# Linear attention and a binarised convolution on one core: keys in pairs, two banks' statistics on ScalarE, stores spread over three queues

## What is computed

```python
def _L0_conv_ref(x, g, b, w_qkv, w_out, b_out):      # 8 heads of 32
    mean, var = jnp.mean(x, axis=1, keepdims=True), jnp.var(x, axis=1, keepdims=True)
    xn = (x - mean) / jnp.sqrt(var + EPS) * g + b    # over the channels
    qkv = jnp.einsum('bchw,oc->bohw', xn, w_qkv).reshape(B, 3, HEADS, DIM_HEAD, N)
    q, k, v = qkv[:, 0] * scale, jax.nn.softmax(qkv[:, 1], axis=-1), qkv[:, 2]
    context = jnp.einsum('bhcn,bhdn->bhcd', k, v)
    out = jnp.einsum('bhcd,bhcn->bhdn', context, q).reshape(B, HEADS * DIM_HEAD, H, W)
    return jnp.einsum('bchw,oc->bohw', out, w_out) + b_out[None, :, None, None] + xn

def _L1_conv_ref(x, W, gamma, beta):
    y = lax.conv_general_dilated(jnp.sign(x), jnp.sign(W), (1, 1), ((1, 1), (1, 1)), ...)  # 3 x 3
    mean, var = jnp.mean(y, axis=(0, 2, 3)), jnp.var(y, axis=(0, 2, 3))
    inv = gamma / jnp.sqrt(var + BN_EPS)
    return (y - mean) * inv + beta + x               # per channel
```

## Time and profile before

| | us |
|---|---|
| median of 3 runs (104.31 to 104.75) | 104.68 |
| profiled execution: its own time | 104.13 |
| profiled execution: its span | 102.3 |

### The profile page before, as it was taken

How to read it: one execution, slowest core, us unless ns; L and a number is a source line. 1 busy time by engine, 2 the same in 40 slices (tenths; PEclk the granted TensorE clock), 3 DMA queues, 4 the chain that set the end, 5 groups by cost and what they waited for, 6 DMA issues and landing times.

```text
span 102.3 us, 2028 instructions
## 1 busy us (share of the span) xinstructions
PE 83.5 (82%) x768; PEld 46.7 (46%) x771; DVE 57.8 (56%) x116; ACT 55.1 (54%) x103; POOL 27.3 (27%) x38
## 2 busy tenths in 40 slices
PE   4999988999997999999999999999999998100000
PEld 4942423556563556455666457565554453100000
DVE  4817959743399345576891684115216299559500
ACT  2246957588894567276792727875214250298000
POOL 6996462462482712082400000000000000005000
PEclk9999999999999999999999999999999999985555
DMA  2997023033000321000240003500800908003993
GB/s 54 308 340 279 10 71 121 0 100 108 0 3 0 103 64 44 0 0 0 72 136 0 0 0 83 128 0 0 205 6 10 201 13 192 0 0 77 319 314 111
DMA packets 4876, 8.89 MB, mean 87 GB/s; under 512 B 1430, under 2 KB 1746, under 8 KB 4868
## 3 DMA queue, kind: packets, MB, share of 16 engines
q1 hardware_dynamic: 3604, 7.59, 25.8%
q10 hardware_dynamic: 1104, 0.66, 2.4%
q0 software_dynamic: 160, 0.52, 1.5%
HBM read 2.51 MB, written 2.10 MB: 45 GB/s over the span
## 4 chain that ended last, share of the span: by engine, by line
PE 69%; DVE 15%; ACT 5%; issue 3%; DVEq 1%
PE ps L791 15%; PE ps L777 8%; PE ps L682 6%; PE ps L778 6%; DVE ST L605 5%; PE ps L849 4%; PE ps L830 3%; PE ps L900 3%; PE ps L743 3%; PE ps L697 3%; PE ps L805 3%; PE ps L812 3%; DVE mxp L532 2%; PE ps L731 2%; PE ps L718 2%
## 5 line engine op out<-in xcount | busy, mean ns | idle before, releaser
L392 ACT ACTIVATE E<-ps 128x512 f32<-128x512 f32 x32 | 18.2, 594 | 5.2 <-PE ps L778 5.2
L532 DVE TENSOR_REDUCE mxp<-ps 128x2 bf16<-128x1024 f32 x12 | 14.7, 1224 | 10.5 <-PE ps L743 10.2
L777 PE MATMUL ps<-wk_max,S 128*128 128x256 bf16 x64 | 15.7, 276 | 0.5 <-ACT wk_max L345 0.5
L791 PE MATMUL ps<-E,XT 128*64 128x256 f32 x128 | 15.6, 385 | 0.0
L778 PE MATMUL ps<-wk_lo,S 128*128 128x256 bf16 x64 | 15.5, 273 | 0.0
L308 POOL DMA_DIRECT2D out<-OUT x2 | 1.3, 674 | 43.2 <-DVE OUT L672 43.2
L791 PEld LDWEIGHTS ps<-E,XT 128*64 128x64 f32 x128 | 8.5, 136 | 4.7 <-issue 0.8
L279 POOL TENSOR_TENSOR x_lo<-XN,x_hi 128x512 bf16<-128x512 f32 x8 | 9.2, 1155 | 2.3 <-DVE x_hi L515 2.2
L321 ACT ACTIVATE sq<-ps 128x512 f32<-128x512 f32 x8 | 4.8, 597 | 8.4 <-PE ps L682 8.4
L682 PE MATMUL ps<-X,center_mat 128*128 128x512 f32 x16 | 9.0, 668 | 0.3 <-DVE XN L509 0.3
L777 PEld LDWEIGHTS ps<-wk_max,S 128*128 128x128 bf16 x64 | 6.2, 97 | 5.9 <-issue 2.8
(11 more groups left out here) (115 smaller groups left out, 130.1 us busy)
## 6 DMA issues: line engine op xcount, KB each, us to landing
X<-in_x SPq DMA_DIRECT2D x3, 512.0 KB, 5.2
X<-X SPq DMA_DIRECT2D x4, 256.0 KB, 3.5
X<-X SPq DMA_DIRECT2D x8, 128.0 KB, 2.4
out<-OUT SPq DMA_DIRECT2D x4, 256.0 KB, 4.1
S<-x_hi SPq DMA_DIRECT2D x7, 126.0 KB
S<-x_lo SPq DMA_DIRECT2D x7, 126.0 KB
X<-in_x SPq DMA_DIRECT2D x2, 256.0 KB, 3.8
out<-OUT POOLq DMA_DIRECT2D x2, 256.0 KB, 4.5
```

Of the source, the lines that this page charges most:

```text
L392: nc.scalar.activation(E[:, b % 2, 2 * g:2 * g + 2, :].rearrange("p k j -> p (k j)"), kt_ps[g % 2], ACT.Exp).then_inc(exp_ready, 1)
L532: nc.vector.tensor_reduce(mxp[:, h, :, t], k_ps, AX.X, ALU.max).then_inc(max_ready, 1)
L777: nc.tensor.matmul(dst, chunk, wk_max[:, b % 2, :], start=True, stop=False)
L791: last = nc.tensor.matmul(d_ps[d * C:d * C + C, :], XT[:, b, k, :], E[:, b % 2, k, :], start=(k < 2), stop=(k >= CH - 2))
```

## The change

TensorE's order: from image 0 on, keys_t is called in pairs (groups 0 and 1, then 2 and 3) with half_keys, project and others between pairs; first_keys(1, 0) stands ahead of keys_t(0, 0); the first rows (pair 0) go to bank 7 and no longer to bank 0, with new waits on the copies that read bank 7; apply_matrix(1) moves from image 7 to the end of image 6. ScalarE's order follows: keep_pt(2) and keep_pt(4) move ahead of the row copies, and the copy of the query and value weights ahead of the second row. VectorE does first_max(1, 0) before normalise(3), and add_input(1) before scale_r(5).

The ending: banks 2 and 3 are no longer among VectorE's statistics. ScalarE reads them in one pass that sums, and in a second that squares the difference from the mean and sums; it writes mean and sum of squares in the form of the statistics' records, whose counts GpSimd writes. SCALED and ADDED begin with banks 4 and 5 singly. The stores are 12 instead of 10: 6 on SP, 5 on GpSimd, 1 on ScalarE.

```diff
-SCALED = ((4, 5), (6, 7), (1,), (0,), (2,), (3,))
-ADDED = ((4, 5), (6, 7), (0, 1), (2,), (3,))
+SCALED = ((4,), (5,), (6, 7), (1,), (0,), (2,), (3,))
+ADDED = ((4,), (5,), (6, 7), (0, 1), (2,), (3,))
+ACT_STATS = (2, 3)
+RECORDS = 4
...
+acc = sb("acc", [P, 3])
+ACC_SUM, ACC_MEAN, ACC_SQUARES = (acc[:, i:i + 1] for i in range(3))
...
+def row_ps(q):
+    return ps[:, 0 if q else 7, 0:HID]
...
-conv_done, y_ready, st_ready = sem("conv_done"), sem("y_ready"), sem("st_ready")
+conv_done, y_ready, st_ready, st_act = sem("conv_done"), sem("y_ready"), sem("st_ready"), sem("st_act")
+st_counts = sem("st_counts")
...
+act_records = ST[:, ACT_STATS[0]:ACT_STATS[-1] + 1, :].rearrange("p b (r e) -> p (b r) e", e=3)
...
-for pair in ((4, 5), (6, 7)):
-    wait_added(sp, pair)
-    sp.dma_start(out_h[0, :, pair[0]:pair[1] + 1, :], OUT[0:C, pair[0]:pair[1] + 1, :]
+for part in ((4,), (5,), (6, 7)):
+    wait_added(sp, part)
+    sp.dma_start(out_h[0, :, part[0]:part[-1] + 1, :], OUT[0:C, part[0]:part[-1] + 1, :]
...
-for q in two:
-    sp.dma_start(out_d[2 * q], OUT[q * C:(q + 1) * C, 0:2, :]).then_inc(stored, 16)
+sp.dma_start(out_d[0], OUT[0:C, 0:2, :]).then_inc(stored, 16)
+wait_added(sp, (2,))
+sp.dma_start(out_d[1, :, 0:BANK], OUT[0:C, 2, :]).then_inc(stored, 16)
...
-sp.wait_ge(stored, 16 * 8)
-sp.wait_ge(stored_pool, 16 * 2)
+sp.wait_ge(stored, 16 * 7)
+sp.wait_ge(stored_pool, 16 * 5)
...
-for pair in ((4, 5), (6, 7)):
-    wait_added(pool, pair)
-    pool.dma_start(out_h[1, :, pair[0]:pair[1] + 1, :], OUT[C:P, pair[0]:pair[1] + 1, :]
+nc.gpsimd.memset(act_records[:, :, 0:1], float(len(ACT_STATS) * BANK // RECORDS)).then_inc(st_counts, 1)
+for part in ((4,), (5,), (6, 7)):
+    wait_added(pool, part)
+    pool.dma_start(out_h[1, :, part[0]:part[-1] + 1, :], OUT[C:P, part[0]:part[-1] + 1, :]
...
+wait_added(pool, (0, 1))
+pool.dma_start(out_d[2], OUT[C:P, 0:2, :]).then_inc(stored_pool, 16)
+wait_added(pool, (3,))
+pool.dma_start(out_d[3, :, BANK:N], OUT[C:P, 3, :]).then_inc(stored_pool, 16)
...
-    nc.scalar.copy(wk_max[d * C:d * C + 1, d, :], ps[d * C:d * C + 1, 0, 0:HID]).then_inc(row_ready, 1)
+    nc.scalar.copy(wk_max[d * C:d * C + 1, d, :], row_ps(b // 2)[d * C:d * C + 1, :]).then_inc(row_ready, 1)
...
-    if b >= 2:
+    if b in (2, 3, 5, 7):
...
-    if b == 1:
-        keep_xt(3)
...
-    if b == 0:
-        keep_xt(1)
+    if b < 2:
+        keep_xt(2 * b + 1)
...
+        query_value_weights()
...
-        query_value_weights()
...
+    if b in (3, 5):
+        keep_pt(b - 1)
...
+nc.scalar.activation(images(OUT, ACT_STATS), images(ps, ACT_STATS), ACT.Copy, accum_out=ACC_SUM
+                     ).then_inc(st_act, 1)
...
+act.wait_ge(st_act, 1)
+act.wait_ge(st_counts, 1)
+nc.scalar.activation(ACC_MEAN, ACC_SUM, ACT.Copy, scale=-1.0 / (len(ACT_STATS) * BANK)).then_inc(st_act, 1)
+nc.scalar.activation(act_records[:, :, 1:2], ACC_SUM.unsqueeze(1).broadcast_to([P, RECORDS, 1]), ACT.Copy,
+                     scale=1.0 / (len(ACT_STATS) * BANK)).then_inc(st_act, 1)
+act.wait_ge(st_act, 2)
+nc.scalar.activation(E[:, 0, 0:CH // 2, :].rearrange("p k j -> p (k j)"), images(ps, ACT_STATS), ACT.Square,
+                     bias=ACC_MEAN, accum_out=ACC_SQUARES).then_inc(st_act, 1)
+act.wait_ge(st_act, 4)
+nc.scalar.activation(act_records[:, :, 2:3], ACC_SQUARES.unsqueeze(1).broadcast_to([P, RECORDS, 1]),
+                     ACT.Copy, scale=1.0 / RECORDS).then_inc(st_act, 1)
...
-for q in two:
-    act.dma_start(out_d[2 * q + 1, :, 0:BANK], OUT[q * C:(q + 1) * C, 2, :]).then_inc(stored, 16)
-wait_added(act, (3,))
-act.dma_start(out_d[3, :, BANK:N], OUT[C:P, 3, :]).then_inc(stored, 16)
+act.dma_start(out_d[3, :, 0:BANK], OUT[C:P, 2, :]).then_inc(stored, 16)
...
+first_max(1, 0)
...
-first_max(1, 0)
...
+half_max(1, 0, 0)
...
-half_max(1, 0, 0)
...
+add_input(1, 0, 2)
...
-add_input(1, 0, 2)
...
-    statistics(j)
-dve.wait_ge(st_ready, B)
+    if j not in ACT_STATS:
+        statistics(j)
+dve.wait_ge(st_ready, B - len(ACT_STATS))
+dve.wait_ge(st_act, 5)
...
-    if d and t == 0:
-        pe.wait_ge(row_ready, 1)
...
-    if h == 0 and t == 0:
+    pe.wait_ge(max_ready, 4 * q + 2 * h + t)
+    if h == 0 and t == 0 and q > 1:
...
-    else:
-        pe.wait_ge(max_ready, 4 * q + 2 * h + t)
...
-        last = nc.tensor.matmul(ps[d * C:d * C + 1, 0, t * P:(t + 1) * P], mx[:, q % 2, d, t:t + 1],
+        last = nc.tensor.matmul(row_ps(q)[d * C:d * C + 1, t * P:(t + 1) * P], mx[:, q % 2, d, t:t + 1],
...
+    pe.wait_ge(wqv_ready if d else wtqv_ready, 1)
...
-    pe.wait_ge(wqv_ready, 1)
+    pe.wait_ge(row_ready, 2)
...
 transpose_x(0)
 variance(3)
 first_row(0)
+first_keys(1, 0)
 keys_t(0, 0)
-first_keys(1, 0)
 center(4)
+first_keys(1, 1)
 keys_t(0, 1)
 transpose_x(1)
-first_keys(1, 1)
 variance(4)
 keys_t(0, 2)
+half_keys(1, 0, 0)
 make_query_value_weights()
 keys_t(0, 3)
+transpose_x(2)
 first_row(1)
-transpose_x(2)
-half_keys(1, 0, 0)
 center(5)
+half_keys(1, 0, 1)
 transpose_out_weights()
 keys_t(1, 0)
+keys_t(1, 1)
 transpose_x(3)
-half_keys(1, 0, 1)
-keys_t(1, 1)
+half_keys(1, 1, 0)
 keys_t(1, 2)
 variance(5)
-half_keys(1, 1, 0)
 keys_t(1, 3)
 make_out_weights()
 half_keys(1, 1, 1)
+transpose_x(4)
 center(6)
-transpose_x(4)
 pair_rows(1)
 context(0)
 keys_t(2, 0)
+keys_t(2, 1)
+variance(6)
 half_keys(2, 0, 0)
-variance(6)
-keys_t(2, 1)
 project(0)
 keys_t(2, 2)
-half_keys(2, 0, 1)
 keys_t(2, 3)
 transpose_x(5)
+half_keys(2, 0, 1)
 context(1)
 center(7)
 keys_t(3, 0)
+keys_t(3, 1)
 half_keys(2, 1, 0)
-keys_t(3, 1)
 project(1)
 keys_t(3, 2)
-half_keys(2, 1, 1)
 variance(7)
 keys_t(3, 3)
+half_keys(2, 1, 1)
 context(2)
 transpose_x(6)
 pair_rows(2)
...
 for b in range(4, B):
     keys_t(b, 0)
+    keys_t(b, 1)
     if b < 6:
         half_keys(3, b % 2, 0)
-    keys_t(b, 1)
     project(b - 2)
     keys_t(b, 2)
+    keys_t(b, 3)
+    if b < 6:
+        half_keys(3, b % 2, 1)
     if b == 5:
         apply_matrix(0)
-    if b < 6:
-        half_keys(3, b % 2, 1)
-    if b == 7:
-        apply_matrix(1)
-    keys_t(b, 3)
+    context(b - 1)
     if b == 4:
         transpose_x(7)
-    context(b - 1)
-    if b == 4:
         transpose_taps()
     if b == 5:
         pair_rows(3)
+    if b == 6:
+        apply_matrix(1)
     if b % 2:
         matrix(b // 2 - 1)
 convolve_first(0, 2)
```

## The result

The changed kernel takes 100.2 us (median of 4 runs) beside 104.5 for the kernel before: a ratio of 0.958, with a 95% interval of 0.952 to 0.964. In a second comparison, with more runs, it was 0.966 (0.960 to 0.972). The profiled execution took 100.34 us (span 98.5) beside 104.13 (102.3). All ratios compare fast executions only (one of the four of the changed kernel, 102.02 us, was in a slower state and is left out), while the only profiles of early_only and pairs_spread are of executions in that state.

A forecast was written before the change was run, and what follows sets the result against it. TensorE's own pieces were taken to bound the kernel up to about 82 us, then a chain of VectorE work and stores. 0.4 + 0.8 + 0 + 0 + 0.9 = 2.1 us gave 102.6 us, range 101.5 to 104.2.

The forecast's parts named there:

- Part 1: TensorE's start up to context(0): first rows in bank 7, first_keys(1, 0) ahead of keys_t(0, 0); 0.4 us, between 0 and 0.8.
- seam: On TensorE: 0.10 us lost whenever the form of the weights in the array changes.
- the 0.19 that I took off the 0.53: At the first rows: keys_t(0, 0) starts 0.19 us later, with 0.53 of work behind it, 0.34 net.
- part 2: From context(0) to convolve_first(0, 2): keys in pairs save ten form changes, 1.0 us; entered as 0.8, bounds 0.5 to 1.2.
- The upper bound of 0.8: The most, in us, that the changed orders up to context(0) were expected to gain.
- What VectorE was to do: Its maxima of pair 1 end late; pair_rows(1) starts at 33.15 after a 0.3 us wait, context(0) at 33.4.
- stalls: TensorE waits of 0.1 to 0.2 us, likely in two or three images after context(0).
- Part 3: Two banks' statistics moved to ScalarE: aggregate only 0.1 us earlier, entered as 0; 0.4 worse to 0.3 better.
- The delay of the last convolution: The summing pass ahead of signs(3) makes convolve(3) begin at 84.5 instead of 83.94.
- Parts 4 and 5: The ending: banks 4 and 5 singly cost nothing, spread stores issue the last one earlier; 0.9 us, between 0.2 and 1.3.
- rival (A): The final stores are bound by the DMA engines, gaining 0.4 us there; total 1.6, 103.1 us; chance 0.20.
- Rival (E): Whole kernel: each part at its good end, 3.6 us in all, 101.1 us; chance 0.06.

The follow-up runs named there:

- early_only: The kernel before with only the orders up to context(0) changed and the first rows in bank 7; 0.988 of before.
- pairs_spread: The changed kernel with banks 4 and 5 scaled, added and stored as a pair again, stores still spread; 0.974 of before.
- log_earlier: The changed kernel with the summing pass behind signs(3), variance(5) ahead of keys_t(1, 2), its logarithm and exponential ahead of exp(1, 2); 0.960 of before.
- project_split: The changed kernel with project of images 0 to 5 cut in two halves, keys_t(b, 2) between them; 0.982 of before.
- singles_unspread: The changed kernel with stores of banks 0 to 3 on the queues of before, banks 4 and 5 still singly; 0.964 of before.
- halves_apart: The changed kernel with half_keys(1, 0, 0) and (1, 0, 1) moved away from neighbours of the same 64x128 form; 0.991 of before.

## Why the prediction was wrong

**Part 1, the step that failed: 0.4, and 1.35 was measured.** The mechanism was right; the dates that I carried were late. Counted from the first keys, I had keys_t(0, 0) at 4.84 (the trace: 4.66), variance(4) at 8.0 (7.7), first_row(1) at 11.8 (11.3), pair_rows(1) at 20.44 (19.53), context(0) at 20.69 (19.74). The last error, 0.95 us, is the whole of the miss in this part.

The first of these dates can be worked again. In the trace of before, first_row(0) starts at 16.64; 0.21 for it and 0.53 for first_keys(1, 0), both from start to start, give 17.38 for keys_t(0, 0), as now. I had 16.96 and 17.55: the 0.10 of a seam was added to distances that contained it already. So the 0.19 that I took off the 0.53 did not exist, and the changes of form around first_keys(1, 0) were not counted. That is why I had 0.34 for a step that is worth 0.81. Seams were also entered where there are none: half_keys to make_query_value_weights and to transpose_out_weights take 0.23 and 0.22 from start to start for 0.22 of work, both forms 64x128. How the rest of the 0.95 is shared out among the steps is not shown.

In part 2 I had counted forms; here I had not, though the count was to be had: from first_row(0) to context(0) 21 changes before and 16 after. At 0.10 to 0.13 these are 0.5 to 0.65. Of the waits that the trace of before lists, 0.45 before keys_t(0, 0), 0.23 before half_keys(1, 1, 1) and 0.29 before center(6) are gone, and about 0.24 before pair_rows(1) is new. Together this makes 1.23 to 1.38, an account that fits 1.35 but was not shown term by term. The upper bound of 0.8 had no row behind it.

**What VectorE was to do** was half right: a wait before pair_rows(1) exists, and log_earlier shows that the chain over the logarithm and normalise(5) sets context(0), as it came 0.31 us earlier. But it waits at a date 0.9 earlier than I had.

**Part 2: right.** 0.96 for ten seams at 0.10; I had entered 0.8, for stalls that did not come. At the 0.13 of project_split ten would be 1.3, so a seam is known to about 0.03. The neighbour steps without 128x128 weights cost too, as counted: half_keys to project, 0.31 for 0.22 of work. The Trainium skill (TensorEngine Tiling (Array Packing), Key Properties) has it that a change of the tiling mode drains TensorE; the trace agrees.

**Part 3: 0 forecast, 0.33 measured.** The sum itself had 0.1 and was entered as 0. The delay of the last convolution was mis-sized: 0.5 by the sum, 0.12 at its weight load, 0.04 at the end of both. From the start of the Y copy to that of the pass, to that of the read-out and to that of signs(3) it was 0.49, 0.91 and 0.10, where I had entered the full durations, 0.58, 1.11 and 0.2. A smaller error went the other way: from that weight load to the first of the last two statistics it is 2.23 (81.48 to 83.71), and I had 2.05. That the 1.2 us of relief do not arrive in full was right.

**Parts 4 and 5: size right (0.9; 1.0 by the clock), reason wrong.** I gave the gain to the last issue, and none to the first store. It is the reverse: pairs_spread has the early last issue and not the gain, singles_unspread has the gain without the spread. As rival (A) had it, the engines are nearly full from shortly after the first store to the end, so the end follows the first store. (A) had priced this at 0.4, from a rate; its own terms (5.0 + 5.7 + 0.7) give T + 11.4 and a gain of 0.7, not T + 11.7. The first store goes 0.96 us earlier relative to T (88.46 - 86.90 = 1.56, before 2.52). Not all of that need arrive: in the changed kernel the engines' share falls to 0.60 and 0.75 in the half microseconds from T + 4.5 to T + 5.5, where additions are awaited. The profiles with the stores of before have 12.15 from T to the end on average, those with the new ones 11.4, so 0.7 is the better estimate by traces. That the size came out at the forecast's 0.9 was luck. The Trainium skill (Trainium Kernel Development and Optimization, Key Constraints) says that several queues only save issue time, which decided more than I let it: the trace agrees, and the issue time saved is worth nothing here (0.964 without the spread).

**The sum**: 2.1 forecast, 3.5 by traces and by the larger comparison; 0.95 of the missing 1.4 is part 1, 0.33 part 3, 0.16 part 2. The other 0.8 up to the 4.3 us of the first comparison is between runs. Rival (E), 3.6 us, comes closest in the sum but not in the parts: part 1 went beyond its 0.8, part 2 and the stores stayed below its 1.2 and 1.3. The range was too narrow upwards, since the bound of part 1 rested on the same dates as its value.

## What to carry to other kernels

Where TensorE is busy throughout, write down its order as a list of weight forms and count the changes; each costs about 0.1 us here, and small products are best put beside others of the same form, as long as VectorE's order still fits (halves_apart lost 2.25 us where it did not). When a tail is full of stores, look first at when the first one can leave. Dates carried by hand must be taken from start to start, and can be checked by carrying the old order in the same way, whose dates are known.

## What was not expected of the hardware

A change of the weights' form costs about 0.1 us also between two forms smaller than 128x128 (64x128 to 128x32: 0.31 from start to start for 0.22 of work), and nothing between two kinds of product with the same 64x128 form (0.22 and 0.23). Reading out ScalarE's accumulator is listed with 0.20 us, but the next instruction began 0.10 after its start. The issue of a store on ScalarE's queue took 1.95 us in singles_unspread, and its T to end is 11.7 beside 11.6 with the spread.
